# Splitting the keys into bf16 parts at the key product, half of them during a path walk

## What is computed

```
x = x + tanh(g_xattn[0]) * dtw_expand(ctx, layernorm(x))       # align each context to its sequence, walk the path back
x = x + tanh(g_ffn[0])   * bitlinear_ffn(layernorm(x))         # ternary weights, depthwise convolution, silu
x = x + tanh(g_xattn[1]) * attention(layernorm(x), ctx, ctx)   # 16 heads of 16
x = x + tanh(g_ffn[1])   * topk_pattern_ffn(layernorm(x))      # three top-k selections, one after the other

# attention, the part that the change touches
k = (ctx @ Wk.T + bk).reshape(B, 375, 16, 16)
scores = einsum('bhqd,bhkd->bhqk', q, k);  softmax;  @ v;  @ Wo.T + bo
```

## Time and profile before

| what | value |
|---|---|
| median of three executions | 578.32 us |
| the profiled execution, its own time | 579.24 us |
| its span in the trace | 577.5 us |
| VectorE busy | 390.5 us (68%) |
| TensorE busy | 390.5 us (68%) |
| ScalarE busy | 280.9 us (49%) |
| GpSimd busy | 85.0 us (15%) |
| forward wave, about | 57 to 112 us of the span |
| join and path walk | 112 to 169 us |
| expand | 171 to 188 us |
| first FFN | 188 to 255 us |

### The profile page before, as it was taken

How to read it: one execution, slowest core, us unless ns; L and a number is a source line. 1 busy time by engine, 2 the same in 40 slices (tenths; PEclk the granted TensorE clock), 3 DMA queues, 4 the chain that set the end, 5 groups by cost and what they waited for, 6 DMA issues and landing times.

```text
span 577.5 us, 10020 instructions
## 1 busy us (share of the span) xinstructions
PE 390.5 (68%) x3338; PEld 267.5 (46%) x3338; DVE 390.5 (68%) x1644; ACT 280.9 (49%) x712; POOL 85.0 (15%) x215
## 2 busy tenths in 40 slices
PE   2898799723249699677898898888999503503106
PEld 2557586511127455445676677676545201103003
DVE  7644999999964768996866566671454575475773
ACT  3854444722231465246676676877443352353440
POOL 6791000000014063720700000000000000000000
PEclk9998699955558799998999999999999955855556
DMA  9700003287004688520044756910950000000002
GB/s 281 222 1 1 0 2 112 102 166 162 20 2 131 92 145 147 151 64 1 2 68 69 201 81 129 213 52 2 374 208 1 0 1 2 1 1 1 1 1 64
DMA packets 33448, 47.22 MB, mean 82 GB/s; under 512 B 5477, under 2 KB 29942, under 8 KB 32246
## 3 DMA queue, kind: packets, MB, share of 16 engines
q1 hardware_dynamic: 33398, 46.58, 33.5%
HBM read 37.87 MB, written 8.60 MB: 80 GB/s over the span
## 4 chain that ended last, share of the span: by engine, by line
PE 43%; DVE 32%; ACT 14%; issue 6%; POOL 4%; DVEq 0%; POOLq 0%; ACTq 0%
PE ps L2133 8%; ACT below L1739 7%; DVE PR L1036 4%; PE ps L1980 4%; PE ps L2097 4%; PE ps L2084 3%; PE ps L2073 3%; PE ps L2059 3%; DVE R L970 2%; PE ps L1925 2%; ACT E L1713 2%; DVE prod L1032 2%; PE ps L1841 2%; DVE PR L1034 2%; PE ps L2255 2%
## 5 line engine op out<-in xcount | busy, mean ns | idle before, releaser
L1250 DVE TENSOR_REDUCE negm<-ps 112x1 f32<-112x375 f32 x128 | 65.2, 544 | 35.7 <-PE ps L2073 35.3
L1713 ACT ACTIVATE E<-ps 125x448 f32<-125x448 f32 x96 | 50.4, 546 | 26.5 <-PE ps L2084 25.5
L2223 PE MATMUL ps<-cnt,same 128*128 128x7 bf16 (+3 forms) x36 | 6.2, 171 | 71.1 <-ACT below L1739 65.1
L2073 PE MATMUL ps<-ks,qs 96*112 96x375 bf16 x128 | 42.0, 340 | 3.6 <-issue 2.3
L1238 DVE TENSOR_REDUCE acts<-gel 128x4 f32<-128x448 f32 x32 | 19.8, 621 | 31.1 <-ACT gel L1670 31.1
L2084 PE MATMUL ps<-qs,ks 99*125 99x112 bf16 x384 | 37.9, 222 | 2.9 <-ACT E L1713 1.0
L2223 PEld LDWEIGHTS ps<-cnt,same 128*128 128x128 bf16 (+1 forms) x36 | 4.0, 111 | 73.9 <-issue 73.9
L2084 PEld LDWEIGHTS ps<-qs,ks 99*125 99x125 bf16 x384 | 33.7, 137 | 9.5 <-ACT E L1713 4.4
L1670 ACT ACTIVATE gel<-ps 128x448 f32<-128x448 f32 x32 | 17.3, 544 | 29.3 <-PE ps L2133 29.3
L767 POOL CAST kp<-kx 128x750 bf16<-128x750 f32 x8 | 6.5, 812 | 163.5 <-ACT path L1584 125.1
L2097 PE MATMUL ps<-E,v 125*32 125x112 f32 x768 | 29.7, 262 | 0.7 <-issue 0.6
(11 more groups left out here) (372 smaller groups left out, 1055.8 us busy)
## 6 DMA issues: line engine op xcount, KB each, us to landing
ks<-key_parts SPq DMA_DIRECT2D x48, 187.5 KB, 6.9
piwT<-fn_process_input_weights SPq DMA_DIRECT2D x4, 2048.0 KB, 14.9
key_parts<-kp SPq DMA_DIRECT2D x48, 93.8 KB
ctx_again<-in_ctx SPq DMA_DIRECT2D x7, 512.0 KB
keys<-kx SPq DMA_DIRECT2D x16, 187.5 KB, 2.1
kx<-keys SPq DMA_DIRECT2D x8, 375.0 KB, 6.0
ctxP<-in_ctx SPq DMA_DIRECT2D x8, 256.0 KB, 6.1
patT<-in_L_ffn_input_patterns SPq DMA_DIRECT2D x1, 2048.0 KB, 14.7
```

The costliest lines, as they stand in the source:

```text
L1250: drain(dve.tensor_reduce(negm[:, n:n + 1], bank(nm)[0:S, 0:SC], AX.X, ALU.max, negate=True), nm)
L1713: drain(fn(E[:, (KCH * f + c) % 6, :], bank(nm)[0:KC, 0:4 * S], ACT.Exp), nm)
L2073: fill(mm(bank(nm)[0:S, 0:SC], qs[0:SR, u // 4 % 3, n, :], ks[0:SR, u // 4 % 3, n, :], start=True, stop=True), nm)
```

## The change

The keys' fp32 round trip through DRAM and GpSimd's splits are dropped. TensorE and ScalarE make the three parts where a unit is produced:

- ScalarE drains `("kT", u)` twice, to fp32 `kx` and to the bf16 high part `kp[:, u % 4, 0]`.
- TensorE makes `("keyMid", u)`: identity times `kx` (fp32) plus `away` (minus identity, bf16) times the high part; ScalarE drains it to bf16 as the middle part. `("keyLow", u)` is the same with two `away` matmuls, minus high and minus middle; its drain is the low part. A key step s holds the product of unit s, the middle of s - 1 and the low of s - 2, on both engines, so there are 18 steps, s from 0 to 17. Steps 0 to 7 stand where the key products stood; steps 8 to 17 stand inside the walk, 1, 2, 2, 2, 1, 1, 1, 0 of them ahead of the groups j = 7 to 0.
- `kx` and `kp` have four slots. From s = 4 ScalarE's step waits until unit s - 4 has been stored (`unit_stored`). SyncE stores a unit in three pieces (`store_unit`): units 0 to 5 ahead of the wait for `tern_ready`, units 6 to 15 after `ctx_again`.
- Names share the banks 0 to 3 in a ring. ScalarE makes `away` after the values are drained, and TensorE's first key step waits for it.

```diff
@@ -28,6 +28,8 @@
 Q_PARTS = (0, 0, 1, 1, 2, 0)
 SR = HD * len(K_PARTS)
 LAG = 5
+KEYS_AHEAD = 8
+KEY_STEPS = (1, 2, 2, 2, 1, 1, 1, 0)
 UP0 = 3
 ACT_ROUNDS = (1, 3, 5)
 
...
@@ -115,8 +117,11 @@
     for b in range(B):
         for c in range(KCH):
             ring(("V", b, c))
-    for u in range(2 * B):
-        p.add(("kT", u), u % 4)
+    n[0] = 0
+    for s in range(2 * B + 2):
+        for i, name in enumerate(("kT", "keyMid", "keyLow")):
+            if 0 <= s - i < 2 * B:
+                ring((name, s - i), (0, 1, 2, 3))
     p.add("joinF", 4)
     p.add("joinG", 5)
     for j in range(7, -1, -1):
...
@@ -292,8 +297,7 @@
         last_stack = rk.at - 2 * NH * SC
         ln0 = Region(rk.at).take("ln0", [S, B, D])
         kx = rk.take("kx", [128, 4, SC])
-        kp_at = rk.at
-        kp = rk.take("kp", [128, 2, 2, 3, SC], BF16)
+        kp = rk.take("kp", [128, 4, 3, SC], BF16)
         v1 = rk.take("v1", [KC, KCH, B, VW])
         rn = Region(rw.at)
         w1n = rn.take("w1n", [128, 2048])
...
@@ -567,10 +570,16 @@
                 sp.dma_start(dst[:, :], src.rearrange("(t p) -> p t", p=128),
                              allow_slow_non_contiguous=True).then_inc(loaded["biasT"], 16)
 
-            for u in range(2 * B):
+            def store_unit(u):
+
                 t, b = u // B, u % B
-                wait_drained(sp, ("kT", u))
-                sp.dma_start(keys[b, 128 * t:128 * t + 128, :], kx[:, u % 4, :]).then_inc(keys_stored[u % 4], 16)
+                wait_drained(sp, ("keyLow", u))
+                for c in range(3):
+                    sp.dma_start(key_parts[b, c, :, 8 * t:8 * t + 8, :].rearrange("d n s -> n d s"),
+                                 kp[:, u % 4, c, :]).then_inc(unit_stored[u % 4], 16)
+
+            for u in range(KEYS_AHEAD - 2):
+                store_unit(u)
 
             sp.wait_ge(tern_ready, 2)
             for kt in range(CT):
...
@@ -585,45 +594,19 @@
 
             def load_stack(b):
 
-                sp.wait_ge(parts_stored[b % 2], 96 * (b // 2 + 1))
+                sp.wait_ge(unit_stored[b % 4], 48 * ((B + b) // 4 + 1))
                 for j, part in enumerate(K_PARTS):
                     sp.dma_start(ks[HD * j:HD * j + HD, b % 3, :, :], key_parts[b, part]).then_inc(stack_loaded[b % 3], 16)
 
-            def load_keys(b):
-
-                if b >= 2:
-                    sp.wait_ge(k_split, b - 1)
-                sp.dma_start(kx[:, 2 * (b % 2):2 * (b % 2) + 2, :], keys[b].rearrange("(t p) s -> p t s", t=2)
-                             ).then_inc(keys_loaded[b % 2], 16)
-
-            def store_parts(b):
-
-                sp.wait_ge(k_split, b + 1)
-                for t in range(2):
-                    for c in range(3):
-                        sp.dma_start(key_parts[b, c, :, 8 * t:8 * t + 8, :].rearrange("d n s -> n d s"),
-                                     kp[:, b % 2, t, c, :]).then_inc(parts_stored[b % 2], 16)
-
-            for i in range(4):
-                sp.wait_ge(keys_stored[i], 64)
-            load_keys(0)
-            load_keys(1)
-            for b in range(2):
-                store_parts(b)
-                load_keys(b + 2)
+            for u in range(KEYS_AHEAD - 2, 2 * B):
+                store_unit(u)
             sp.wait_ge(x_ready, B)
             sp.wait_ge(consts_ready, 1)
             for b in range(3):
                 sp.dma_start(ks[SR:SR + 3, b, :, :], onesb[0:3, :].unsqueeze(1).broadcast_to([3, NH, SC])
                              ).then_inc(loaded["ones_k"], 16)
-            for b in range(2):
+            for b in range(3):
                 load_stack(b)
-            for b in range(2, B):
-                store_parts(b)
-                if b + 2 < B:
-                    load_keys(b + 2)
-                if b == 2:
-                    load_stack(2)
             for b in range(3, B):
                 wait_filled(sp, ("scoreT", 4 * b - 9, KCH - 1))
                 load_stack(b)
...
@@ -758,26 +741,6 @@
                                     float((m + 1) * STEPS[r]) - (0.5 if m >= VC else 0.0)))
             settle()
 
-            def split_keys(b):
-
-                x32, part = kx[:, 2 * (b % 2):2 * (b % 2) + 2, :], kp[:, b % 2, :, :, :]
-                pool.wait_ge(keys_loaded[b % 2], 16 * (b // 2 + 1))
-                if b >= 2:
-                    pool.wait_ge(parts_stored[b % 2], 96 * (b // 2))
-                did(pool.tensor_copy(part[:, :, 0, :], x32))
-                settle()
-                did(pool.tensor_tensor(x32, x32, part[:, :, 0, :], ALU.subtract))
-                settle()
-                did(pool.tensor_copy(part[:, :, 1, :], x32))
-                settle()
-                pool.tensor_tensor(part[:, :, 2, :], x32, part[:, :, 1, :], ALU.subtract).then_inc(k_split, 1)
-
-            wait_drained(pool, ("path", 0))
-            for b in range(2):
-                split_keys(b)
-            wait_drained(pool, ("ffn_up", 0, 1))
-            for b in range(2, B):
-                split_keys(b)
             for t in range(2):
                 wait_drained(pool, ("qT", t, 1))
                 far = slice(448, 896)
...
@@ -1554,12 +1517,27 @@
                     drain(fn(v1[:, c, b, 0:NH * (HD + 1)].rearrange("p (h e) -> p h e", e=HD + 1)[:, :, 0:HD],
                              bank(nm)[0:KC, 0:D].rearrange("p (h e) -> p h e", e=HD), ACT.Copy), nm)
             act.wait_ge(loaded["biasT"], 48)
-            for u in range(2 * B):
-                nm = ("kT", u)
-                wait_filled(act, nm)
-                if u >= 4:
-                    act.wait_ge(keys_stored[u % 4], 16 * (u // 4))
-                drain(fn(kx[:, u % 4, :], bank(nm)[:, 0:SC], ACT.Identity, bias=bkT[:, u // B:u // B + 1]), nm)
+            fn(away[:, :], identb[:, :], ACT.Copy, scale=-1.0).then_inc(away_ready, 1)
+
+            def key_step(s):
+
+                if s < 2 * B:
+                    nm = ("kT", s)
+                    wait_filled(act, nm)
+                    if s >= 4:
+                        act.wait_ge(unit_stored[s % 4], 48 * (s // 4))
+                        wait_filled(act, ("keyLow", s - 4))
+                    bias = bkT[:, s // B:s // B + 1]
+                    did(fn(kx[:, s % 4, :], bank(nm)[:, 0:SC], ACT.Identity, bias=bias))
+                    drain(fn(kp[:, s % 4, 0, :], bank(nm)[:, 0:SC], ACT.Identity, bias=bias), nm)
+                for c, name in enumerate(("keyMid", "keyLow")):
+                    u = s - 1 - c
+                    if 0 <= u < 2 * B:
+                        wait_filled(act, (name, u))
+                        drain(fn(kp[:, u % 4, 1 + c, :], bank((name, u))[:, 0:SC], ACT.Copy), (name, u))
+
+            for s in range(KEYS_AHEAD):
+                key_step(s)
             act.wait_ge(winv_ready, 1)
             for i, w in enumerate((w1n, w2n)):
                 did(fn(w[:, :], w[:, :], ACT.Identity, bias=magic[:, 0:1], scale=winv[:, i:i + 1]))
...
@@ -1575,6 +1553,9 @@
                 act.wait_ge(traced, T - t0)
                 fn(turned[0:64, t0:t1, :], hand(PR[0:64, t0, 2 * RB + 1:2 * RB + 2], [[PW, t1 - t0], [-2, RB]]),
                    ACT.Copy).then_inc(turned_ready, 1)
+                at = KEYS_AHEAD + sum(KEY_STEPS[0:7 - j])
+                for s in range(at, at + (KEY_STEPS[7 - j] if j >= 0 else 0)):
+                    key_step(s)
                 nm = ("path", j + 1)
                 if j == 7:
                     continue
...
@@ -1873,14 +1854,30 @@
                         ins = mm(bank(nm)[0:KC, 0:D], ctxT[:, h, b, KC * c:KC * c + KC], wvT[:, h, :],
                                  start=(h == 0), stop=(h == DH - 1))
                     fill(ins, nm)
-            for u in range(2 * B):
-                nm = ("kT", u)
-                t, b = u // B, u % B
-                claim(pe, nm)
-                for h in range(DH):
-                    ins = mm(bank(nm)[:, 0:SC], wkT[:, h, 128 * t:128 * t + 128], ctxT[:, h, b, :],
-                             start=(h == 0), stop=(h == DH - 1))
-                fill(ins, nm)
+            def key_step(s):
+
+                if s < 2 * B:
+                    nm = ("kT", s)
+                    t, b = s // B, s % B
+                    claim(pe, nm)
+                    for h in range(DH):
+                        ins = mm(bank(nm)[:, 0:SC], wkT[:, h, 128 * t:128 * t + 128], ctxT[:, h, b, :],
+                                 start=(h == 0), stop=(h == DH - 1))
+                    fill(ins, nm)
+                for c, name in enumerate(("keyMid", "keyLow")):
+                    u = s - 1 - c
+                    if 0 <= u < 2 * B:
+                        nm = (name, u)
+                        claim(pe, nm)
+                        wait_drained(pe, ("keyMid", u) if c else ("kT", u))
+                        mm(bank(nm)[:, 0:SC], ident[:, :], kx[:, u % 4, :], start=True, stop=False)
+                        for part in range(c + 1):
```

(18 more changed lines are left out.)

## The result

Four executions of the changed kernel took 586.55 to 589.53 us, median **588.75**; the kernel before took 578.05 beside them. The ratio is 1.0183, 95% interval 1.0146 to 1.0219: the change makes the kernel 1.8% slower, 0.45 us from the forecast. The profiled execution took 588.76 us, its span is 587.1 against 577.5.

What follows compares the result with a forecast made beforehand. No one engine bounds the kernel (TensorE 43% of the chain); VectorE alone paces the walk. Late expand +14.4, splits -4.4, together +10.0 on 579.24 gives 589.2, less 0.9 to the median: 588.3 us; range 576 to 597.

Steps and rivals of the forecast that it cites:

- The keys before the join: Key steps 0 to 7 take 21.9 us against 20.33, plus 0.9 waiting for `away`; VectorE's join held by 1.9 us.
- SyncE's order: `store_unit(6)` stands behind SyncE's issuing of `ctx_again`, 119.4 to 142.2; unit 6's last issue starts at 143.4.
- The landing: Unit 6's store lands 2.5 us after its last issue, at 146.0; upper bound 5.0, so 148.4.
- ScalarE's idle time: In the walk, ScalarE idles some 8 us before a `kx` drain, waiting for unit 6's store, ending near 146.
- The late groups: After group 6, each group costs its key steps plus 2.3 us hand-over; expand starts at 185.15, 14.4 us later.
- The clock: TensorE's clock 0.50 near 145, 1.00 from about 156, low again as the expand starts, which keeps 17.10 us.
- rival 2: TensorE's clock never rises in the late groups: +25.3 us, 603.6; half of that 596; chance 0.12.
- The splits' removal: First FFN: small VectorE operations no longer lengthened beside GpSimd's splits, a gain of 4.4 us (bounds 3.5 and 4.8).
- Rival 1: The walk stays on time, unit 6 landing by about 134 to 136.5: 575.8, or 572.7 at high clock; chance 0.18.

Runs made afterwards that it cites:

- experiment 1: The changed kernel with the stores of units 6 to 15 issued from GpSimd's queue instead of SyncE's: 572.41 us, ratio 0.9898 to the kernel before.
- experiment 2: The changed kernel without the loads of the last two of `ctx_again`'s four slices, stores still behind it on SyncE: 574.81 us in one timed execution.
- Experiment 4: The changed kernel with `ctx_again`'s nine loads issued from GpSimd's queue, all key stores on SyncE with nothing ahead: 583.92 us, ratio 1.0107.
- experiment 3: The kernel before with GpSimd's four split operations per batch replaced by one tiny copy, keys' loads and stores kept: 570.47 us, ratio 0.9874.
- experiment 6: The kernel before with `ctx_again`'s load of 46 rows cut into 32 and 14 rows: 576.95 us, ratio 0.9994.
- experiment 9: The changed kernel with units 6 to 15 stored from GpSimd's queue and the 46-row loads cut into 32 and 14: 575.07 us, ratio 0.9962.

## Why the prediction was right, point by point

- **The keys before the join.** Forecast: first product 0.9 us late, end at 110.7, the join read 1.9 us late. Measured: 0.8 (88.64 against 87.87), 110.26, and 1.24. The bf16 matmuls of 375 columns were 0.16 and not 0.18.
- **SyncE's order.** `ctx_again` from 119.09 to 141.92 (forecast 119.4 to 142.2), unit 6's last issue at 143.60 (143.4). Right; experiment 1 shows that this order holds the key step up, and experiment 2 agrees.
- **The landing: the term that was mis-sized.** Forecast 2.5 us with an upper bound of 5.0; measured from 143.60 to 150.32, which is 6.7. The 2.5 came from an idle queue, and for most of the store it was nearly right: 21 of its 27 increments had come after 3.0 us. The other six came from two engines, by all signs those that were still at the 46-row load, and a store counts as landed only with the last of them. The forecast has no term for that tail, though it spoke of the issue on line 583, which the same load holds up. The 5.0 us of the earlier trace rows were kept for the bound alone. Experiment 4 had 20 us. A store's landing depends on what is still in the DMA engines, not only on the queue's order.
- **ScalarE's idle time** was forecast at 8 us ending at 146 and is 14.03 ending at 150.39: 4.3 of the excess is the landing, the rest comes from its start, since ScalarE was through with step 9 at 136.4 and not at 138.
- **The late groups.** Forecast 11.5, 8.5, 5.4, 4.1, 3.3 and 2.65 us; measured from each last `turned` matmul to the next 11.1, 8.3, 5.3, 4.0, 3.2 and 2.7. The sum of steps plus hand-over was right to 3%. From the landing to the expand it was 37.4 us where 39.15 had been forecast, so of 4.3 us of late landing 2.6 reached the expand: 17.0 instead of 14.4.
- **The clock.** (The prediction read its fall in the kernel before as 115.7; 0.73 in the earlier trace rows puts it at 115.5, which changes no term.) It was 0.50 in 149 to 150, where it had been forecast low, and 0.91 in 159 to 160, 5.8 us after TensorE had started again at 153.36 (forecast 6). It then stayed at 1.00 through the groups, though TensorE was idle for 1.06 us in each hand-over: rival 2 did not occur. It fell again just before the expand, as forecast, and this took 16.80 us (17.10).

```profile
149.00:150.00 1.00, 0.00 (x0) 0.00 (x0) 0.90 (x7) 0.00 (x0) 0.00 (x0) 0.50 0.14 38
...
159.00:160.00 1.00, 1.00 (x6) 0.60 (x4) 0.93 (x5) 0.48 (x1) 0.00 (x0) 0.91 0.06 16
```

- **The splits' removal.** Forecast -4.4, measured -4.8 from the last add of the expand to the first add behind the down product; experiment 3, which takes nothing else of the keys' way out, has -5.6, with a somewhat higher clock. The Trainium skill ("SBUF — State Buffer", section "SBUF: two separate sides") says that the port pair which VectorE shares with GpSimd is an exclusive lock: of a GpSimd operation and a VectorE operation that needs the pair, the one that starts first has it for its whole instruction., where VectorE's operations end just after GpSimd's, and 0.17 us without splits agree with it; which VectorE operations need the pair was not tested.
- **A gain that wasn't forecast.** Between the first add behind the down product and the pattern products the distance shrank by 2.1 us. In the kernel before TensorE's clock fell at the start of the attention, and there it did not after:

```profile
268.00:270.00 2.00, 1.37 (x15) 1.09 (x13) 1.65 (x4) 0.54 (x1) 0.00 (x0) 0.77 0.04 8
270.00:272.00 2.00, 2.00 (x15) 1.81 (x14) 1.24 (x3) 0.54 (x1) 0.00 (x0) 0.50 0.00 0
```

These are rows of the kernel before; in the kernel after 278 to 284 us, the same products, have 1.00 throughout. In experiment 3 it is 1.00 there too, with the keys' loads and stores unchanged, and so it is in every other profiled execution without splits; experiment 6, which has them, shows 0.66 from 266 to 276 us. So it comes with the splits, but by what path a split or its absence moves the clock 20 us later was only argued and not shown.

The errors cancelled: +2.6 up to the expand, -0.3 in it, -0.4 in the FFN, -2.3 from the attention on. The forecast of 588.3 was right in its mechanism and partly lucky in its size: a late landing and a gain in the attention, neither of them in the sum, nearly cancelled. Its own range to 597 allowed for a late landing, though for 2.4 us and not for 4.3. Rival 1 named the deciding point rightly: with unit 6 stored by 134 to 136.5 the walk stays on time, at 572.7 to 575.8. In experiment 1 it was stored by 135.7 and the time was 572.4.

## What to carry to other kernels

Work that is moved under another engine's stretch is nearly free only if each wait that it brings is free too: look up what stands ahead of its transfers in the issuing queue, and what is in the DMA engines then, and take the landing time from a row with that traffic. When an engine issues a transfer for 12 us, look at the DMA share beside it; here one of 0.14 meant two engines and a size that doesn't divide well. What is stored behind such a load waits for the same two engines. And a gain on one stretch has to be followed to the next: here a kept clock shortened the expand by 1.7 us, and a lower clock after it took that back. The low stretches of the clock move from one version to the next, and one of four us at 0.57 is worth up to 1.7, so look for them before a difference of 2 us is given another cause.

## What the runs showed of the hardware that was not expected

- A load of 46 rows of 8 KB moves at 46 GB/s once it is alone, and the next issue on SyncE, of only 18 rows, stands behind it for 12.3 us. With 32 and 14 rows that issue takes 0.7 us, and the traffic is at 155 GB/s from 139 to 142 us, where it had been at 46.
- Stores of 94 KB from GpSimd's queue land in 2.7 us when the DMA engines are partly free (experiment 1, 139 to 142 us) and in 9 amid the traffic; from SyncE's queue in 6.7 behind the end of `ctx_again`, of which 3.8 are two engines' tail, and in 20 when GpSimd's queue holds the large loads. Which queue holds the small transfers and which the large ones, with the packets that go with it, made a difference of 11 us.
- Spreading a load better over the DMA engines can make a kernel slower: in experiment 9 it took the gap in which small stores had slipped through (DMA share 1.11 instead of 0.72 from 138 to 142 us), and the expand started 1.8 us later.
